# Sorted expert layer of a 12-layer decoder: down weights held in SBUF, rows loaded by fours, placing matmuls in bf16, and the last two batches' gathers and sums moved into the next stage

## The chip, the cores and the metric

The kernel runs on one core of a Trainium2 chip. The metric is the device time of one execution in microseconds (us). The core has TensorE (PE: matmuls; its weight loads are shown apart as PEld), VectorE (DVE), ScalarE (ACT), GpSimd (POOL) and SyncE (SP, which here only issues DMAs). POOL issues the indirect DMAs (gathers and scatters by a list of row numbers).

## The reference, cut to what matters

Twelve residual layers act on `x` of 4 batches x 512 tokens x 128 features. The third and the fourth matter here.

```python
def _L0_ffn_ref(x, gate_w, gate_b, w1, b1, w2, b2):      # 8 experts, top 2
    gate_logits = jnp.einsum('bsd,de->bse', x, gate_w) + gate_b
    weights, indices = jax.lax.top_k(gate_logits, TOP_K)
    weights = jax.nn.softmax(weights, axis=-1)
    h = jnp.einsum('bsd,edh->ebsh', x, w1) + b1[:, None, None, :]
    xh, gh = jnp.split(h, 2, axis=-1)
    act = jax.nn.silu(gh) * xh
    out_e = jnp.einsum('ebsf,efd->ebsd', act, w2) + b2[:, None, None, :]
    out_e = jnp.transpose(out_e, (1, 2, 0, 3))
    sel = jnp.take_along_axis(out_e, indices[..., None], axis=2)
    return jnp.sum(sel * weights[..., None], axis=2)

x = x + _L0_ffn_ref(_layernorm(x), ...)     # the sorted expert layer
x = x + _L1_attn_ref(_layernorm(x), ...)    # a gated scan along the tokens, per batch
```

The next layer, cross attention over 32 context tokens, shares a stage with the scan.

## The kernel before, in words

`x`, `y` and `a` live in SBUF, features on the 128 partitions, 2048 tokens along the free side; a batch is 512 columns (`sl(b)`). The program is a row of stages; each ends with a barrier over all engines, and at some of them the semaphores are cleared too. Within a stage every engine runs its own list in the order in which the code stands, and waits on semaphores; nothing is reordered.

`layer2` is the sorted expert layer. It computes only the two chosen experts of each token. Batches 0 and 1 are group 0, batches 2 and 3 group 1.

- *Choosing and placing.* TensorE centres the tokens and computes the gate logits; DVE ranks the experts (`choose`) and writes a 0/1 matrix `oh` of the chosen ones. `place(g)` counts with one matmul against a triangular matrix and eight against ones how many earlier tokens chose the same expert. DVE's `locate(g)` turns this into `where` (the row of each token and choice in a list that is sorted by expert, each expert's part filled up to a multiple of 128) and into `first_row` (for each tile of 128 rows the row at which its expert's weights begin in DRAM). POOL then scatters the normalised tokens, 16 indirect DMAs per group, into the DRAM tensor `sorted`.
- *The expert loop.* There are 23 tiles of 128 rows per group, N = 46 in all. For tile n: `turn` transposes four tiles at once on TensorE, ACT copies them (`lay`); `inner(n)` does four gate and four up matmuls, ACT applies Silu, DVE multiplies (`hidden`), `down(n)` does four down matmuls, DVE evicts (`evict`), and SP stores the 128 result rows to DRAM (`results`). TensorE's order is: turn of the next four (at n % 4 = 1), `inner(n)`, `down(n-1)`, and at n = 2, 4, 6, 8 a `flip` of the mixing weights of one batch (four small transposes).
- *Weights.* `ring(n)` is a ring of four slots in the big SBUF buffer. SP's `fetch(n)` reads the tile's expert from `first_row` and loads gate, up and down weights and biases, 128 x 1544 floats. `fetch(n+4)` waits for `down(n)`. On SP's queue it is followed by the store of tile n, which waits for its eviction.
- *Rows.* `bring(0)` loads four tiles, then the other 19 of group 0; `bring(1)`, at n = 10, loads the 23 tiles of group 1 in one DMA.
- *Coming back.* When a group's results are stored, POOL gathers for each of its 8 token tiles the two rows (16 indirect DMAs). `mix(b)` on DVE weights and adds them (eight instructions), `join(b)` on TensorE transposes them and adds the bias product (10 passes), `add(b)` on DVE adds to `x`. Batches 0 and 1 do this inside the expert loop, at n = 36 and 41; batches 2 and 3 (`last`) after it.

`layers_3_and_4` is the next stage. For each batch: `centre` (TensorE), `square` (ACT), `variance` (TensorE), `invert` (ACT: two Ln, two Exp), `normed` (DVE: `a` and `y`), POOL's `x += y`, `project_in` (four matmuls), `sigmoids` (ACT, with another function table), `scan` (DVE), `project_out` (TensorE), `add` (DVE). The batches are interleaved by the order of the code. Cross attention follows. The buffer `big` is 18,432 columns wide; `load_big` fills it in later layers, and `k.big_loaded` counts these loads.

Of the kernel before, what the change touches and what calls it, by code (L numbers as in the profile page):

```python
# [8 lines left out]
ALU = mybir.AluOpType  # L9
ACT = mybir.ActivationFunctionType  # L10
AX = mybir.AxisListType
F32 = mybir.dt.float32
# [10 lines left out]
MAGIC = 12582912.0  # L23
EXPERT_GROUPS = ((0, 1), (2, 3))
# [752 lines left out]
def layer2(nc, k, x, y, a):  # L777
# [5 lines left out]
    G, C, SLOTS, FOUR, W_COLS = 8, 4, 4, 4, 12 * P + 8  # L783
# [5 lines left out]
    turns = -(-N // FOUR)  # L789
    MIX_AT = {firsts[g + 1] + 13 + 5 * i: b for g, group in enumerate(EXPERT_GROUPS[:-1]) for i, b in enumerate(group) if firsts[g + 1] + 13 + 5 * i < N - 1}  # L790
    last = [b for b in range(B) if b not in MIX_AT.values()]
    names = ("bias_in counted numbered folded cg_ready zeroed centred squared summed rooted rs_ready logits chosen placed mapped normed exps shifted weighed "
             "positions turned laid gate up silu hidden down evicted flipped flat mixed joined done chain "
             "w_0 w_1 w_2 w_3 scattered_0 scattered_1 x_first x_in_0 x_in_1 stored_0 stored_1 stored_2 stored_3 got_0 got_1 got_2 got_3")
    rows_in, rows_out = k.sorted_rows, [nc.dram_tensor(f"results_{nc.next_id()}", (n * P, D), F32).ap() for n in limits]
    with ExitStack() as mem, stage(nc, names) as (block, s):
        sb = lambda n, w_, dt=F32: mem.enter_context(nc.sbuf_tensor(f"{n}_{nc.next_id()}", [P, w_], dt))
        cg, sq, var, b2, w8t = sb("cg", G), sb("sq", 2 * S), sb("var", NT), sb("b2", P), sb("w8t", T)
# [5 lines left out]
        where, spot, first_row, share = sb("where", 2 * NT, I32), sb("spot", 2 * NT), sb("first_row", N, I32), sb("share", 2 * NT)  # L804
        xt, out, o = sb("xt", 2 * S), sb("out", 4 * P), sb("o", 2 * S)
# [8 lines left out]

        @block.sync
        def _(sp):
            def fetch(n):
                g = group_of(n)
                sp.wait_ge(s["mapped"], g + 1)
# [4 lines left out]
            def bring(g):  # L824
                sp.wait_ge(s[f"scattered_{g}"], 16 * 2 * len(blocks[g]))
                for lo, hi, loaded in ((0, FOUR, "x_first"), (FOUR, limits[0], "x_in_0")) if g == 0 else ((0, limits[g], f"x_in_{g}"),):
                    dst = k.big[:, (firsts[g] + lo) * P:(firsts[g] + hi) * P].rearrange("p (n d) -> p n d", d=D)
                    sp.dma_start(dst, rows_in[g][lo * P:hi * P, :].rearrange("(n p) d -> p n d", p=P)).then_inc(s[loaded], 16)
# [6 lines left out]
            fetch(SLOTS - 1)  # L835
            for n in range(N):
                if n == 10 and len(EXPERT_GROUPS) > 1:
                    bring(1)
                if n + SLOTS < N:
                    fetch(n + SLOTS)  # L840
                g = group_of(n)
                sp.wait_ge(s["evicted"], n + 1)
                sp.dma_start(rows_out[g][sl(n - firsts[g], P), :], out[:, sl(n % 4, P)]).then_inc(s[f"stored_{n % 4}"], 16)
# [2712 lines left out]
```

## Time and profile before

| | us |
|---|---|
| three executions | 2023.61, 2015.76, 2008.88 |
| median | 2015.76 |
| the profiled execution | 2025.27 |
| its span on the core | 2023.2 |
| mean granted clock of TensorE, share of full | 0.928 |

| engine | busy us | share of the span | instructions |
|---|---|---|---|
| PE | 1777.6 | 88% | 20105 |
| PEld | 1285.1 | 64% | 20124 |
| DVE | 1241.8 | 61% | 2434 |
| ACT | 1056.1 | 52% | 2386 |
| POOL | 834.2 | 41% | 1087 |

How to read it: shares are averages over some fifty stages with different limits. A stage is read from the order of time in it: who waits last and for whom. A row of the timeline has the start in us, the duration of the whole group, the engine, the line of the kernel, the operation, out<-in with the shapes, how many instructions are in the group, and in brackets how long the engine stood idle before it and what released it. An fp32 matmul appears as two passes, each with a weight load.

### The profile page before, as it was taken

To read this page: it belongs to the slowest core of one execution; us is meant where nothing else is said; L and a number is where in the kernel's file an instruction comes from. 1 tells how busy PE (TensorE), PEld (TensorE's weight loads), DVE (VectorE), ACT (ScalarE), POOL (GpSimd) and SP (SyncE) were. 2 spreads that over 40 slices of the span, in tenths; PEclk is the share of its full clock that TensorE was granted. 3 is DMA by queue.
4 is the path that set the end of the run, shared out by engine and by line. 5 is a ranking of instruction groups with operands and counts; after the bars stand their busy time and mean duration, and the time that the engine had idled before them with its cause. 6 is when DMAs were issued, how large, how long until landed. Compare 5 with 4: busy or idle time off the path is not lost. (4 is left out here: it accounts for less than half of the span.)

```text
span 2023.2 us, 50650 instructions
## 1 busy us (share of the span) xinstructions
PE 1777.6 (88%) x20105; PEld 1285.1 (64%) x20124; DVE 1241.8 (61%) x2434; ACT 1056.1 (52%) x2386; POOL 834.2 (41%) x1087
## 2 busy tenths in 40 slices
PE   7784899485699999999999788999999999999885
PEld 4333898243457888888888536888788856633332
DVE  4544345259657777777674327887888777734434
ACT  4551443267686666666664344555555541066552
POOL 1004120305357776767662104666666620044201
PEclk9996999695799999999999798999999998799998
DMA  6003887000041000000000314444444300000100
GB/s 236 1 1 98 288 274 243 24 1 0 1 154 38 14 24 14 24 14 24 14 22 16 153 47 120 126 131 135 125 125 132 119 1 1 1 1 1 38 1 22
DMA packets 46846, 141.84 MB, mean 70 GB/s; under 512 B 11112, under 2 KB 17648, under 8 KB 45840
## 3 DMA queue, kind: packets, MB, share of 16 engines
q1 hardware_dynamic: 42704, 131.20, 20.0%
q0 software_dynamic: 2816, 7.21, 1.1%
q8 instruction: 164, 2.69, 0.5%
q14 instruction: 74, 0.61, 0.1%
q10 hardware_dynamic: 1088, 0.13, 0.0%
HBM read 120.43 MB, written 18.09 MB: 68 GB/s over the span
## 5 line engine op out<-in xcount | busy, mean ns | idle before, releaser
L2510 DVE SCALAR_TENSOR_TENSOR big<-bank,pack,big 128x256 f32<-128x256 f32 (+2 forms) x384 | 182.9, 477 | 41.6 <-ACT mask L2399 25.4
L1958 DVE TENSOR_TENSOR hl<-bank,hh 128x512 fp32r<-128x512 f32 x192 | 132.8, 692 | 64.6 <-ACT hh L1892 55.1
L1892 ACT ACTIVATE hh<-bank 128x512 fp32r<-128x512 f32 x192 | 114.9, 598 | 94.0 <-DVE bank L1953 90.9
L2398 ACT ACTIVATE big<-bank,pack 128x256 f32<-128x256 f32 x192 | 90.6, 472 | 127.8 <-PE bank L2206 123.4
L772 PE MATMUL bank<-yh,wl 128*128 128x512 f32 x384 | 151.4, 394 | 5.3 <-DVE yl L1902 2.5
L773 PE MATMUL bank<-yl,wh 128*128 128x512 f32 x384 | 150.6, 392 | 0.0
L774 PE MATMUL bank<-yh,wh 128*128 128x512 f32 x384 | 150.2, 391 | 0.0
L1792 POOL TENSOR_TENSOR a<-a,rep 128x512 f32<-128x512 f32 x96 | 125.0, 1302 | 30.7 <-DMA rep<-routing 25.6
L1953 DVE TENSOR_TENSOR bank<-bank,a 128x512 f32<-128x512 f32 x192 | 133.2, 694 | 6.6 <-POOL a L1792 0.9
L2910 ACT ACTIVATE pt<-bank 128x1024 f32<-128x1024 f32 (+3 forms) x128 | 79.5, 706 | 99.1 <-PE bank L2762 99.0
L2116 POOL TENSOR_TENSOR big<-big,mask 128x256 f32<-128x256 f32 (+1 forms) x128 | 93.7, 732 | 90.3 <-DVE big L2510 58.1
L2692 POOL TENSOR_SCALAR_AFFINE_SELECT pt<-pt 128x256 f32<-128x256 f32 x128 | 54.9, 440 | 175.4 <-ACT pt L2910 173.1
L2206 PE MATMUL bank<-y,pack 128*128 128x262 f32 (+1 forms) x384 | 120.5, 399 | 5.1 <-DVE big L2510 4.8
L2193 PE MATMUL bank<-big 128*128 128x128 f32 x896 | 123.6, 286 | 0.0
L1781 POOL CAST wh<-big 128x384 fp32r<-128x384 f32 x96 | 48.6, 506 | 169.3 <-PE bank L774 114.6
L2193 PEld LDWEIGHTS bank<-big 128*128 128x128 f32 x896 | 107.8, 192 | 5.2 <-issue 1.4
L1092 DVE SCALAR_TENSOR_TENSOR a<-bank,big,a 128x128 f32<-128x128 f32 x184 | 51.8, 344 | 95.4 <-ACT a L1005 87.1
L2936 DVE TENSOR_REDUCE part<-bank 128x8 f32<-128x1024 f32 (+1 forms) x80 | 93.9, 1219 | 24.5 <-PE bank L2742 23.7
L1783 POOL TENSOR_TENSOR wl<-big,wh 128x384 fp32r<-128x384 f32 x96 | 98.3, 1024 | 7.7
L2742 PE MATMUL bank<-big 32*128 32x128 f32 (+1 forms) x1024 | 92.6, 355 | 4.2 <-DVE part L2936 4.2
L2742 PEld LDWEIGHTS bank<-big 32*128 32x128 f32 x1024 | 74.3, 222 | 33.0 <-issue 18.8
L1005 ACT ACTIVATE a<-bank,big 128x128 f32<-128x128 f32 x184 | 52.5, 368 | 74.2 <-PE bank L904 73.8
(597 smaller groups left out, 4551.2 us busy)
## 6 DMA issues: line engine op xcount, KB each, us to landing
big<-in_experts SPq DMA_DIRECT2D x46, 772.0 KB, 4.7
rep<-routing SPq DMA_DIRECT2D x64, 384.0 KB, 3.5
rep<-routing SPq DMA_DIRECT2D x64, 256.0 KB, 4.0
big<-in_big SPq DMA_DIRECT2D x1, 9216.0 KB, 25.7
gate<-big SPq DMA_DIRECT2D x32, 256.0 KB, 2.0
z<-gate SPq DMA_DIRECT2D x16, 512.0 KB
rep<-routing SPq DMA_DIRECT2D x64, 128.0 KB, 3.6
pack<-in_pack SPq DMA_DIRECT2D x1, 5846.5 KB, 21.2
```

The source lines that it names most:

```text
L772: nc.tensor.matmul(out, pl, dh[:, cur], start=start, stop=False)
L773: nc.tensor.matmul(out, ph, dl[:, cur], start=False, stop=False)
L774: return nc.tensor.matmul(out, ph, dh[:, cur], start=False, stop=stop)
L1783: nc.gpsimd.tensor_tensor(low, src, high.bitcast(F32), ALU.subtract).then_inc(s["w_low"], 1)
L1792: nc.gpsimd.tensor_tensor(spread_(m), spread_(m), spread(n), ALU.mult).then_inc(s["odd"], 1)
L1892: nc.scalar.activation(hh[:, sl((n - 1) % 3)], up_bank(n - 1), ACT.Copy).then_inc(s["high"], 1)
L1953: nc.vector.tensor_tensor(up_bank(n), up_bank(n), other, ALU.mult).then_inc(s["h"], 1)
L1958: nc.vector.tensor_tensor(hl[:, sl(n % 3)], up_bank(n), hh[:, sl(n % 3)].bitcast(F32), ALU.subtract).then_inc(s["low"], 1)
L2193: mm4 = lambda out, gr, left_, right: [nc.tensor.matmul(out[:, sl(h % GH, P)], left_(h), right(h), start=True, stop=True) for h in hs(gr)][-1]
L2206: nc.tensor.matmul(haloed(i)[:, :, 3 - halo:], k.w["L2_attn_qkv_w"][:, sl(m, P)], tokens, start=True, stop=True).then_inc(s["raw"], 1)
L2510: ins = nc.vector.scalar_tensor_tensor(out=d, in0=conv_in(i, back), scalar=weight(i, 3 - back), in1=d, op0=ALU.mult, op1=ALU.add)
L2742: mm = nc.tensor.matmul(both(at)[:, gl * S + c * w:][:, 0:w], qj[b][rows, j * S + i * P:][:, 0:P], kd[b][rows, key:key + w], start=kind != ...
```

## The change

- The down weights of all eight experts (`big0`, 128 x 4096 floats, 2 MB) are loaded once, at the program's start, into columns 14336 to 18431 of `big`, as the last DMA of that stage on SP. A fetch now brings 128 x 1032 floats. `down(n)` reads the weights at a column that stands in a register: `first_col`, written by DVE beside `first_row`, is loaded by TensorE into 23 registers per group (`address(0)` ahead of the loop, `address(1)` at n = 4). `fetch(n+4)` waits for `hidden(n)`.
- Rows are loaded four tiles at a time, `bring(q)`, two turns ahead.
- `oh`, the triangle and the ones are bf16 in `place`; POOL writes the two bf16 copies.
- The flips move to n = 5, 7, 9, 11, and DVE's `weigh` to n = 1 and 3 of the loop.
- For batches 2 and 3 the gathers, `mix`, `join` and `add` move into the next stage: POOL issues the sixteen gathers ahead of its `x += y`; the batches there are centred one after the other, each after its late sum.

```diff
-    G, C, SLOTS, FOUR, W_COLS = 8, 4, 4, 4, 12 * P + 8
+    G, C, SLOTS, FOUR, W_COLS = 8, 4, 4, 4, 8 * P + 8
...
-        oh = [sb("oh", (len(bs) + 1) * G) for bs in blocks]
+        oh = [sb("oh", (len(bs) + 1) * G, BF16) for bs in blocks]
+        later_bf, ones_bf = sb("later_bf", P, BF16), sb("ones_bf", P, BF16)
...
+        down_weights = k.big[:, BIG0_AT:BIG0_AT + G * C * P]
...
+        def collect(pool, b):
+            g = [b in group for group in EXPERT_GROUPS].index(True)
+            for slot in range(4):
+                pool.wait_ge(late.s[f"stored_{slot}"], 16 * len(range(slot, firsts[g + 1], 4)))
+            for t in range(TB * b, TB * b + TB):
+                for i in range(2):
+                    nc.gpsimd.indirect_dma_start(out=found(t, i), out_offset=None, in_=rows_out[g], in_offset=bass.IndirectOffsetOnAxis(where[:, i * NT + t:][:, 0:1], 0)).then_inc(late.s[f"got_{b}"], 16)
...
             def fetch(n):
-                after(sp, s["down"], n - SLOTS + 1)
+                after(sp, s["hidden"], C * (n - SLOTS + 1))
...
+            def bring(q):
+                for g in range(len(blocks)):
+                    lo, hi = max(FOUR * q, firsts[g]), min(FOUR * (q + 1), firsts[g + 1])
+                    if lo < hi:
+                        sp.wait_ge(s[f"scattered_{g}"], 16 * 2 * len(blocks[g]))
+                        src = rows_in[g][(lo - firsts[g]) * P:(hi - firsts[g]) * P, :].rearrange("(n p) d -> p n d", p=P)
+                        sp.dma_start(k.big[:, lo * P:hi * P].rearrange("p (n d) -> p n d", d=D), src).then_inc(s[f"x_{q % 3}"], 16)
...
             bring(0)
             fetch(SLOTS - 1)
+            bring(1)
             for n in range(N):
-                if n == 10 and len(EXPERT_GROUPS) > 1:
-                    bring(1)
                 if n + SLOTS < N:
                     fetch(n + SLOTS)
+                if n % FOUR == 0 and n // FOUR + 2 < turns:
+                    bring(n // FOUR + 2)
+                store(n)
...
+            def address(g):
+                held = [pe.alloc_register(f"column_{n}_{nc.next_id()}") for n in range(firsts[g], firsts[g + 1])]
+                pe.wait_ge(s["addressed"], g + 1)
+                pe.load(held, first_col[0:1, 32 * g:32 * g + limits[g]])
+                columns.extend(pe.snap(r, min_val=0, max_val=(G - 1) * C * P) for r in held)
...
-                    mm = nc.tensor.matmul(down_bank(n), h(n, c), ring(n)[:, sl(2 * C + c, P)], start=c == 0, stop=c == C - 1)
+                    mm = nc.tensor.matmul(down_bank(n), h(n, c), down_weights[:, bass.ds(columns[n] + c * P, P)], start=c == 0, stop=c == C - 1)
...
         @block.gpsimd
         def _(pool):
+            for b in late.batches:
+                late.collect(pool, b)
             for b in range(B):
                 pool.wait_ge(s["y_ready"], b + 1)
...
+            def late_rows(b):
+                pe.wait_ge(s["kcopied"], 1)
+                late.join(pe, b)
+                pe.wait_ge(late.s["done"], b + 1)
...
             scan(0)
             scan(1)
+            late.mix(dve, 2)
             add(0)
+            late.add(dve, 2)
+            add(1)
             normed(2)
-            add(1)
+            scan(2)
+            late.mix(dve, 3)
+            late.add(dve, 3)
+            add(2)
             normed(3)
-            scan(2)
             scan(3)
-            add(2)
             add(3)
...
+                sp.dma_start(k.big[:, BIG0_AT:BIG0_AT + ap["big0"].shape[1]], ap["big0"]).then_inc(k.big_loaded, 16)
```

On TensorE's list, the expert loop's tiles 2 and 3 in the kernel before (L904 gate, L908 up, L915 down, L922 flip; each row is an instruction of the program, x4 four in a row):

```order
L904 MATMUL bank<-xt,big 128x128 x4
L908 MATMUL bank<-xt,big 128x128 x4
L915 MATMUL bank<-big,a 128x128 x4
L922 MATMUL bank<-pack,w_1486 8x128 x4
L904 MATMUL bank<-xt,big 128x128 x4
L908 MATMUL bank<-xt,big 128x128 x4
L915 MATMUL bank<-big,a 128x128 x4
```

The same place in the kernel after (L948 gate, L952 up, L965 down, L958 the register load of group 1): tile 3's gate and up, the down matmuls of tile 2, and the start of tile 4:

```order
L948 MATMUL bank<-xt,big 128x128 x4
L952 MATMUL bank<-xt,big 128x128 x4
L965 ISA
L965 MATMUL bank<-big,a 128x128
L965 ISA
L965 MATMUL bank<-big,a 128x128
L965 ISA
L965 MATMUL bank<-big,a 128x128
L965 ISA
L965 MATMUL bank<-big,a 128x128
L958 TENSOR_LOAD first_col
L959 ISA x3
```

Each down matmul has a register instruction (ISA) ahead of it, and one load of 23 registers stands between the down matmuls of tile 2 and the gate matmuls of tile 4.

On POOL's list, from the scatters (L859) to the adds of the next stage (L1163), before (L865 the gathers; L46 and L37 the end of the stage):

```order
L859 DMA sorted<-y,where 2944x128 x32
L865 DMA big<-results,where 128x128 x32
L46 UNCONDITIONAL_BRANCH
L37 ISA
L1159 UNCONDITIONAL_BRANCH
L1163 TENSOR_TENSOR x<-x,y 128x512 x4
```

And after (L906 the scatters, L828 the gathers, L1203 the adds):

```order
L906 DMA sorted<-y,where 2944x128 x32
L828 DMA big<-results,where 128x128 x16
L47 UNCONDITIONAL_BRANCH
L38 ISA x2
L1197 UNCONDITIONAL_BRANCH
L828 DMA big<-results,where 128x128 x16
L1203 TENSOR_TENSOR x<-x,y 128x512 x4
```

Sixteen of the thirty-two gathers stand behind the stage's end now, ahead of the four adds.

On TensorE's list in the scan stage, before (L1169 centre, L1174 variance, L1179 and L1185 the products of project_in, L1194 project_out):

```order
L1179 MATMUL bank<-a,pack 128x512 x2
L1169 MATMUL bank<-x,pack 128x512
L1179 MATMUL bank<-a,pack 128x512
L1185 MATMUL bank<-a,pack 128x512
L1179 MATMUL bank<-a,pack 128x512 x2
L1169 MATMUL bank<-x,pack 128x512
L1174 MATMUL bank<-sq,pack 128x512
L1194 MATMUL bank<-h,pack 128x512
L1174 MATMUL bank<-sq,pack 128x512
L1194 MATMUL bank<-h,pack 128x512
```

And after (L1209 centre, L1214 variance, L1219 and L1225 project_in, L1234 project_out, L833 and L835 the join):

```order
L1234 MATMUL bank<-h,pack 128x512
L833 MATMUL bank<-w8t,b_1441 128x512
L835 MATMUL bank<-pack,o 128x128 x4
L1209 MATMUL bank<-x,pack 128x512
L1214 MATMUL bank<-sq,pack 128x512
L1234 MATMUL bank<-h,pack 128x512
L1219 MATMUL bank<-a,pack 128x512
L1225 MATMUL bank<-a,pack 128x512
L1219 MATMUL bank<-a,pack 128x512 x2
L833 MATMUL bank<-w8t,b_1441 128x512
L835 MATMUL bank<-pack,o 128x128 x4
L1209 MATMUL bank<-x,pack 128x512
```

Batches 2 and 3 each have a join ahead of their centre, and batch 3's centre stands behind batch 2's products.

## Rows read from the trace of the kernel before

**Rows 1.** Stretches: busy us (count) per engine, granted clock, DMA share, GB/s.

```profile
198.50:353.00 154.50, 141.86 (x1178) 136.95 (x1178) 65.92 (x247) 62.62 (x201) 27.58 (x29) 0.96 0.81 270
355.00:386.00 31.00, 8.12 (x20) 4.55 (x20) 5.89 (x18) 0.00 (x0) 15.21 (x16) 0.54 0.12 36
388.00:440.00 52.00, 43.12 (x115) 18.89 (x115) 23.14 (x34) 35.70 (x55) 5.08 (x4) 0.96 0.00 0
```

**Rows 2.** Timeline: group 0's placing matmuls, and POOL's first scatter.

```profile
166.66 0.67 PE L884 MATMUL bank<-oh,pack 128*128 128x72 f32 x2 [1.13 <-DVE oh L1031]
167.13 3.52 PE L887 MATMUL bank<-oh,pack 128*128 128x64 f32 x16
173.76 1.08 POOL L859 DMA_INDIRECT sorted<-y,where  x1 [15.15 <-DVE where L1065]
```

**Rows 3.** Groups by line, TensorE: busy us, mean ns | idle before.

```profile
L1523 PE MATMUL bank<-q2w,q2t 128*128 128x128 bf16 x64 | 8.0, 285 | 0.4 <-ACT q2t L1613 0.3
L915 PE MATMUL bank<-big,a 128*128 128x128 f32 x368 | 49.6, 278 | 0.5 <-DVE a L1092 0.5
```

**Rows 4.** Timeline, TensorE: tile 1's turn.

```profile
205.00 0.63 PE L894 MATMUL bank<-pack,big 128*128 128x128 f32 x4 [0.86 <-DMA big<-sorted]
```

**Rows 5.** Timeline, TensorE: gate groups of tiles 1, 37, 38, 44, 45.

```profile
205.46 1.06 PE L904 MATMUL bank<-xt,big 128*128 128x128 f32 x8
...
322.40 1.06 PE L904 MATMUL bank<-xt,big 128*128 128x128 f32 x8
...
327.22 1.06 PE L904 MATMUL bank<-xt,big 128*128 128x128 f32 x8
...
347.10 1.06 PE L904 MATMUL bank<-xt,big 128*128 128x128 f32 x8
...
349.78 1.06 PE L904 MATMUL bank<-xt,big 128*128 128x128 f32 x8
```

**Rows 6.** Timeline, SP and TensorE: around the second group's rows, gates of tiles 13, 14, 16.

```profile
237.08 0.72 SPq L828 DMA_DIRECT2D big<-sorted  x1
...
238.76 4.83 SPq L822 DMA_DIRECT2D big<-in_experts  x1
...
241.43 1.13 PE L904 MATMUL bank<-xt,big 128*128 128x128 f32 x8 [0.15 <-issue]
...
249.35 2.05 PE L904 MATMUL bank<-xt,big 128*128 128x128 f32 x8 [5.00 <-issue]
...
257.59 1.06 PE L904 MATMUL bank<-xt,big 128*128 128x128 f32 x8
```

**Rows 7.** The fetches: three first on the timeline; line L822's durations and landing.

```profile
174.75 2.83 SPq L822 DMA_DIRECT2D big<-in_experts  x3
...
L822 SPq FUSED_REGOPS  x46: 37/37/48, 174.6 to 342.7; - x46
DMA to landing us min/median/max: 4.2/4.7/10.5
```

**Rows 8.** Timeline: from tile 45's eviction to the scan stage's last add.

```profile
354.31 0.29 DVE L1097 COPY out<-bank 128x128 f32<-128x128 f32 x1 [1.05 <-PE bank L915]
356.87 0.95 POOL L865 DMA_INDIRECT big<-results,where  x1 [49.75 <-DMA results<-out]
...
368.22 0.28 DVE L1105 TENSOR_SCALAR o<-big,share 128x128 f32<-128x128 f32 x1 [13.62 <-DMA big<-results,where]
...
375.71 0.95 POOL L865 DMA_INDIRECT big<-results,where  x1 [0.31 <-issue]
...
385.43 0.69 DVE L1111 TENSOR_TENSOR x<-x,bank 128x512 f32<-128x512 f32 x1 [4.23 <-PE bank L932]
...
387.96 3.75 PE L1169 MATMUL bank<-x,pack 128*128 128x512 f32 x4 [2.56 <-PEq L38]
...
403.35 0.69 DVE L1389 TENSOR_TENSOR h<-h,gt 128x512 f32<-128x512 f32 x1
...
426.58 0.69 DVE L1394 TENSOR_TENSOR x<-x,bank 128x512 f32<-128x512 f32 x1 [1.28 <-PE bank L1194]
```

More of the change, by code:

```diff
@@ L23 @@
 MAGIC = 12582912.0
+BIG0_AT = 14336
 EXPERT_GROUPS = ((0, 1), (2, 3))
@@ L813, in layer2, with join, mix, add @@
         mine = lambda m, g, w_=G: m[:, blocks[g][0] * w_:(blocks[g][-1] + 1) * w_]
+        def collect(pool, b):
[5 more added lines that the diff above has]
+                    nc.gpsimd.indirect_dma_start(out=found(t, i), out_offset=None, in_=rows_out[g], in_offset=bass.IndirectOffsetOnAxis(where[:, i * NT + t:][:, 0:1], 0)).then_inc(late.s[f"got_{b}"], 16)
+        def join(pe, b):
+            pe.wait_ge(late.s["mixed"], b + 1)
+            after(pe, late.s["done"], b)
+            nc.tensor.matmul(k.ps[7], b2[0:G, :], w8t[0:G, sl(b)], start=True, stop=False)
+            for i in range(TB):
+                mm = nc.tensor.matmul(k.ps[7][:, sl(i, P)], o[:, b % 2 * S + i * P:][:, 0:P], k.ident, start=False, stop=i == TB - 1)
+            mm.then_inc(late.s["joined"], 1)
+        def mix(dve, b):
+            dve.wait_ge(late.s[f"got_{b}"], 16 * 2 * TB)
+            after(dve, late.s["joined"], b - 1)
+            for i in range(TB):
+                t = TB * b + i
+                cur = o[:, b % 2 * S + i * P:][:, 0:P]
+                nc.vector.tensor_scalar(cur, found(t, 0), share[:, t:t + 1], None, ALU.mult).then_inc(late.s["scaled"], 1)
+                dve.wait_ge(late.s["scaled"], t + 1)
+                mixed = nc.vector.scalar_tensor_tensor(out=cur, in0=found(t, 1), scalar=share[:, NT + t:][:, 0:1], in1=cur, op0=ALU.mult, op1=ALU.add)
+            mixed.then_inc(late.s["mixed"], 1)
+        def add(dve, b):
+            dve.wait_ge(late.s["joined"], b + 1)
+            nc.vector.tensor_tensor(x[:, sl(b)], x[:, sl(b)], k.ps[7], ALU.add).then_inc(late.s["done"], 1)
+        late.collect, late.join, late.mix, late.add, late.batches = collect, join, mix, add, last
         @block.sync
@@ L923, in flip @@
                 mm.then_inc(s["flipped"], 1)
-            def join(b):
-                pe.wait_ge(s["mixed"], b + 1)
-                pe.wait_ge(s["flat"], B)
-                pe.wait_ge(s["bias_in"], 16)
-                after(pe, s["done"], b)
-                nc.tensor.matmul(k.ps[7], b2[0:G, :], w8t[0:G, sl(b)], start=True, stop=False)
-                for i in range(TB):
-                    mm = nc.tensor.matmul(k.ps[7][:, sl(i, P)], o[:, b % 2 * S + i * P:][:, 0:P], k.ident, start=False, stop=i == TB - 1)
-                mm.then_inc(s["joined"], 1)
+            columns = []
             nc.tensor.matmul(k.ps[7][:, 0:G], k.w["centre"], k.w["L0_ffn_gate_w"], start=True, stop=True).then_inc(s["folded"], 1)
@@ L943, in _ @@
             pe.wait_ge(s["normed"], B)
+            address(0)
+            pe.wait_ge(k.big_loaded, 16)
             turn(0)
             for n in range(N + 1):
+                if n == 4 and len(blocks) > 1:
+                    address(1)
                 if n % FOUR == 1 and n // FOUR + 1 < turns:
@@ L1121, in _ @@
                 shifted(g)
-            for g in range(len(EXPERT_GROUPS)):
-                weigh(g)
             for n in range(N + 1):
+                if n in (1, 3) and n // 2 < len(EXPERT_GROUPS):
+                    weigh(n // 2)
                 if n < N:
@@ L1129, in _, with layers_2_to_4, layers_3_and_4 @@
                 if n in MIX_AT:
-                    mix(MIX_AT[n])
+                    mix(dve, MIX_AT[n])
                 if n - 2 in MIX_AT:
-                    add(MIX_AT[n - 2])
-            for i, b in enumerate(last):
-                mix(b)
-                if i:
-                    add(last[i - 1])
-            add(last[-1])
-            dve.wait_ge(s["done"], B)
-def layers_3_and_4(nc, k, x, y, a):
+                    add(dve, MIX_AT[n - 2])
+            dve.wait_ge(s["evicted"], N)
+def layers_2_to_4(nc, k, x, y, a):
+    late = Kit()
+    names = "stored_0 stored_1 stored_2 stored_3 got_0 got_1 got_2 got_3 scaled mixed joined done"
+    late.s = {n: nc.alloc_semaphore(f"{n}_{nc.next_id()}") for n in names.split()}
+    with ExitStack() as mem:
+        layer2(nc, k, x, y, a, mem, late)
+        layers_3_and_4(nc, k, x, y, a, late)
+    counted.extend(late.s.values())
+def layers_3_and_4(nc, k, x, y, a, late):
     sems = ("centred squared var ln inv y_ready a_ready mixed keys values kcopied vcopied gates value sig driven gated proj summed "
```

114 lines of the change are left out of this document (53 added, 61 removed).

## Prediction

> **What bounds the kernel now.** I read the page first for the whole, then the busy time by stretch, then the order of time from 158 us (the sorted expert layer begins) to 428 us (the scan of the next stage ends). Everything the change touches lies there; the other 1,750 us I take as unmoved. Three things are to be seen. In the expert loop (198.5 to 353 us) TensorE is busy 141.9 of 154.5 us with its clock almost always at the upper level, 2.4 GHz (granted 0.96), while the DMA engines are busy 0.81 of the time: TensorE bounds it, DMA is close behind [rows 1]. Between 355 and 386 us almost nothing works but POOL, which issues sixteen gathers; TensorE is busy 8.1 of 31 us at the lower level, 1.2 GHz (0.54) [rows 1]. Before the loop, POOL's scatters wait until DVE has written `where`, and DVE waits for the placing matmuls [rows 2].
>
> **The loop's stalls.** The gate matmuls of two neighbouring tiles start 347.10 and 349.78: 2.68 us for 24 weight-and-matmul passes, 0.112 us each [rows 5]. The 45 gate groups from tile 1 (205.46) to tile 45 (349.78) span 144.3 us. Without stalls it would be 44 x 2.68 = 117.9; ten turns and four flips of four passes, 14 x 0.45 = 6.3; two joins, the first of which stretches a step from 2.68 to 4.82 (2.1), the second taken as 2.6, so 4.7. That makes 128.9, so **15.4 us are stalls**. Over half is one event: SP issues the whole second group's rows at 237.08 (1.4 MB in 512-byte rows), its next fetch is stuck in issue for 4.83 us, and tile 14's gate starts 7.92 us after tile 13's, after 5.00 us of idleness; by tile 16 the loop is 16.16 us from tile 13 where 8.04 would do: 8.1 us lost, part of it because TensorE's clock fell to the lower level after the idle time (the gate group at 249.35 takes 2.05 us, the one at 257.59 1.06) [rows 6]. The rest is weights that land late: a fetch needs 4.7 us (4.2 to 10.5) to land [rows 7] and is issued only after `down(n)`.
>
> **The change, part by part** (gains positive).
> 1. *Places in bf16.* Per group one L884 and eight L887 matmuls, 18 passes in fp32, from 166.66 to 170.65: 4.0 us [rows 2]. In bf16 they are 9 passes. Bounds: half of it, 2.0; or nine at 8.0/64 = 0.125 us, the bf16 row of 128x128 [rows 3], 1.1, so 2.9 saved. That row is the nearer in type, but it stands at the upper clock level and this stretch at the lower: I take 2.6. For group 0 it is on the path (place, `where`, first scatter at 173.76, the rest of the scatters, first rows). Group 1's copy is hidden, since POOL is busy with group 0's scatters until about 194. The extra `first_col` instruction and the two bf16 copies on POOL lie beside waits. **+2.6** (2.0 to 2.9).
> 2. *Rows by fours.* Tile 1's turn waited 0.86 us for the 19-tile load [rows 4]; it goes, but the turn then comes nearer to the low clock of the start: **+0.5** (0 to 0.9). The second group's 23-tile burst disappears altogether.
> 3. *Down weights in SBUF.* A fetch falls from 772 to 516 KB. It no longer waits for `down(n)` but for `hidden(n)`. The SP queue still has `store(n-1)` ahead of it, so it comes only about 1 us sooner. With a transfer two thirds as long, the weights that were late by tenths come over 1 us early. The 2 MB load at the start sits at the end of SP's queue, 150 us ahead of its use: 0, covered by layers 0 and 1. With the burst and the lateness both gone I take 14 of the 15.4: **+14** (8 to 15.4; 8 if only the burst goes).
> 4. *Registers on TensorE.* Two `TENSOR_LOAD`s of 23 registers. The first stands in the 12 us in which TensorE waits for rows: 0. The second stands in the loop ahead of tile 4 and stops what is queued behind it, tile 4's gate. The trace has only SP's load of one register: three fetches in 2.83 us, (2.83 - 0.33)/2 - 0.33 - 0.04 = 0.88 us each [rows 7]. Bounds: 0.88 for the lot, or 23 x 0.88 = 20. About 2 us is covered, because the sequencer gets there when `hidden(2)` is done while the third down group is still to run. So the cost is 0 to 18; the nearest row is one load instruction, so I stay near it but not on it: **-3**.
>  The Trainium skill (Runtime: NRT & Kernel Launch, Instruction fetch mechanics) speaks against this edit: a register load costs some 200 ns per register even in bulk, by which each load would be an estimated 4.6 us and the second would cost 2.6. No row of this case shows a bulk load.
> 5. *A register operation ahead of each down matmul*, 4 x 46 = 184. SP's takes 37 ns [rows 7]: 0 if TensorE's sequencer runs ahead, 6.8 us if not. `hidden(n)` is ready about 1.2 us before its down group's turn, longer than four such operations: **0**.
>  The Trainium skill (TensorE: Matmul & The Clock Gate, Architectural detail) gives TensorE's queue a depth of 64, by which a step's instructions are ahead of the array; that too makes it 0.
> 6. *The last two batches inside the scan stage.* Before: tile 45's eviction ends at 354.59, the first gather starts at 356.87, the mix at 368.22, the last sum ends at 386.12, the new stage starts at 387.96, and its last `add` ends at 427.27: 72.7 us after the eviction [rows 8]. After: 1.8 us of barrier, then from the stage's start 0.5 + 16 x 1.256 = 20.6 us until POOL has issued the gathers (fifteen steps from 356.87 to 375.71). Behind them on POOL stand its own adds `x += y` (5.08/4 = 1.27 each [rows 1]), which DVE's `add(0)` needs, and behind `add(0)` on DVE stands `late.add(2)`, which `centre(2)` on TensorE needs: centre(2) at about 23.7. Batch 0 in the trace goes from centre (387.96) to gated (404.04) in 16.1 us, with the keys' work and four microseconds of low clock in it [rows 8]; alone on fast matmuls its own instructions sum to about 11. I take 12. Then batch 3's mix (eight instructions, 2.6), join (2.1, as in the loop) and add (0.7), 5.4 together, its chain 12, its output product and add 2: 23.7 + 12 + 5.4 + 12 + 2 = 55.1; with 16.1 twice, 63.3. One batch at a time leaves TensorE gaps, so I put 58. 72.7 - 1.8 - 58 = 12.9, less 1 since the second normalisation now starts right behind the last batch instead of beside it: **+12** (6 to 15).
>
> Sum: 2.6 + 0.5 + 14 - 3 + 0 + 12 = **26 us**. Against the profiled execution's 2025.3 us that is 1999; it stands 9.5 us above the median of three, 2015.8 (range 2008.9 to 2023.6), so I forecast 2015.8 - 26 = **1990 us**.
>
> **Rivals.**
> A. *POOL's queue and the clock eat the overlap.* If centre(2) waits as worked out and TensorE's clock stays at the lower level through both chains, item 6 gives 6 or less: 1996 to 1999. For it: the stretch with sparse TensorE work had 0.54; against: from 388 on, with gaps of 1 to 2 us, it had 0.96 [rows 1].
> B. *Registers load one after another.* Item 4 costs 18 instead of 3, with a fall of the clock behind the idle time: 2006. For it, the only load in the trace costs 0.88 us; against, it is a single instruction.
> C. *More arrives*: the bulk load is hidden and item 6 gives 15: 1983 to 1978.
> D. *Slower.* A down matmul whose address stands in a register may not start until the pass before it has ended. A pass lasts 278 ns [rows 3] and its neighbours start every 112: 0.166 x 368 = 61 us more, 2015.8 - 26 + 61 = 2051. It decides from 26/368 = 0.07 us a pass. No row shows a matmul with a register address; against it, no wait in this trace hangs on how an address was made.
> E. *The loop was not held by its loads*: a rhythm of 2.68 us with the same stalls. Against it: the stalls sit exactly behind the burst. It would give 2004.
>
> **Chances.** Forecast 0.56, A 0.14, B 0.12, C 0.09, D 0.05, E 0.04. The forecast's own range is 1980 to 1999. The range for 8 in 10, which takes in A and C and part of B: 1976 to 2005. About 1% (20 us) is what a measurement of this kernel can tell from no change: 1995.6 is that line. Faster takes 0.47 of the forecast, all of C and half of A: 0.63. Slower by over 1% is D: 0.05. Same 0.32.
>
> **What would show it.** Right: the gate groups 2.68 us apart without a gap near tile 14; the first scatter 2.6 us sooner; gathers issued beside the scan stage's first matmuls; `centre(2)` released by DVE's sum about 24 us after the stage begins; the eviction of tile 45 to the stage's last add in about 60 us. Wrong: a TensorE gap over 3 us ahead of tile 4 (B); down groups longer than 1.06 us (D); the granted clock at 0.5 for most of the scan stage (A); fetches still landing late (E).

## The result, and the profile after

| | before | after |
|---|---|---|
| executions | 20 | 20 |
| median, us | 2010.32 | 1995.89 |
| lowest to highest, us | 1999.85 to 2025.28 | 1986.62 to 2010.86 |
| the profiled execution, us | 2025.27 | 1993.77 |
| its span, us | 2023.2 | 1992.0 |

The ratio over all executions is 0.9941, 95% interval 0.9918 to 0.9964 (0.9928 between the two medians): 0.6 to 0.7% faster, less than the 1% that a measurement tells from no change. The direction and the range of the forecast held, its size did not: 14 us between the medians instead of 26. The same pair gave 0.9894 (0.9856 to 0.9932) and 0.9916 (0.9881 to 0.9951) in two further comparisons (e1 and e10 below), so all three lie below 1.

The two profiled executions lie 31 us apart, more than twice as much as the medians. By stage, each from its start to the next one's, in us:

| stretch | before | after | |
|---|---|---|---|
| start of `layer2` to the first gate group | 42.4 | 39.2 | -3.2 |
| first gate group to tile 45's eviction | 154.2 | 139.7 | -14.6 |
| tile 45's eviction to the end of the scan and cross attention stage | 94.0 | 93.1 | -0.9 |
| sum | 290.6 | 271.9 | -18.7 |
| one attention layer late in the program | 331.4 | 316.0 | -15.4 |
| all the rest | 1401.2 | 1404.1 | +2.9 |

The attention layer's code is untouched. Its largest group by line of before, and then of after (busy us, mean ns | idle before):

```profile
L2742 PE MATMUL bank<-big 32*128 32x128 f32 (+1 forms) x1024 | 92.6, 355 | 4.2 <-DVE part L2936 4.2
```

```profile
L2794 PE MATMUL bank<-big 32*128 32x128 f32 (+1 forms) x1024 | 80.8, 314 | 4.1 <-DVE part L2988 4.1
```

In before's trace TensorE's granted clock is 0.77 from 1665 to 1785 us, so it stands for part of the layer at 1.2 GHz; in after's it is 0.93. Over all thirteen traces of the study this mean is 314 or 315 ns in seven, 332 in one and 345 to 355 in five, with either kernel on either side. So that part is not the change's; it belongs to the execution. **The change's own share is the 18.7 us**, which came out as 18.5 in a second pair of traces.

*Ahead of the loop*, timeline of after (start, duration, engine, line, operation, [idle before, releaser]):

```profile
166.09 0.19 PE L928 MATMUL bank<-oh,later_bf 128*128 128x72 bf16 x1 [1.13 <-DVE oh L1077]
166.12 0.35 PE L931 MATMUL bank<-oh,ones_bf 128*128 128x64 bf16 x8
...
167.06 0.21 DVE L1102 TENSOR_TENSOR full<-bank,number 128x64 f32<-128x64 f32 x1
...
170.06 1.08 POOL L906 DMA_INDIRECT sorted<-y,where  x1 [11.56 <-DVE where L1111]
```

The placing matmuls take 0.4 us where they took 4.0 [rows 2]; DVE no longer waits for them, and the first scatter comes 12.6 us after the layer's start instead of 15.8.

*The loop.* TensorE's rows by line (duration ns min/median/max), and the fetches' landing:

```profile
L958 PEldq TENSOR_LOAD <-first_col x2: 2329/2432/2535, 179.5 to 207.5; - x2
...
L965 PE MATMUL bank<-big,a x368: 275/275/372, 202.7 to 335.6; 128*128 x184
L965 PEldq FUSED_REGOPS  x184: 46/46/56, 201.7 to 335.1; - x184
...
DMA to landing us min/median/max: 3.4/4.1/5.9
```

Timeline, TensorE: ahead of tile 4, and the gates of tiles 13 and 16:

```profile
208.06 1.06 PE L965 MATMUL bank<-big,a 128*128 x8
210.79 1.13 PE L948 MATMUL bank<-xt,big 128*128 128x128 f32 x8 [1.68 <-issue]
...
238.04 1.06 PE L948 MATMUL bank<-xt,big 128*128 128x128 f32 x8
...
246.08 1.06 PE L948 MATMUL bank<-xt,big 128*128 128x128 f32 x8
```

Tiles 13 to 16 are 8.04 us apart, without a gap, where before lost 8.1 [rows 6]. A fetch lands after 4.1 us instead of 4.7, and never later than 5.9 instead of 10.5 [rows 7]. The one idle time over 0.6 us in the loop is that of the register load ahead of tile 4. The down matmul whose address stands in a register has a median of 275 ns, which is also the median of before (mean 278 [rows 3]).

*The last two batches*, busy us per engine, granted clock, DMA share and GB/s by stretch, and the timeline:

```profile
338.40:358.20 19.80, 16.36 (x36) 6.90 (x36) 7.31 (x10) 12.89 (x20) 14.51 (x15) 0.85 0.18 46
358.20:369.00 10.80, 4.20 (x11) 2.43 (x11) 6.83 (x12) 0.94 (x1) 3.44 (x3) 0.64 0.05 14
369.00:383.00 14.00, 9.47 (x14) 2.87 (x14) 4.77 (x7) 7.14 (x10) 1.26 (x1) 0.79 0.00 0
383.00:394.00 11.00, 7.91 (x15) 4.04 (x16) 2.81 (x10) 0.81 (x2) 0.00 (x0) 0.60 0.00 0
```

```profile
335.95 0.29 DVE L1144 COPY out<-bank 128x128 f32<-128x128 f32 x1 [1.14 <-PE bank L965]
...
338.39 3.75 PE L1209 MATMUL bank<-x,pack 128*128 128x512 f32 x4 [2.48 <-PEq L39]
...
339.15 0.95 POOL L828 DMA_INDIRECT big<-results,where  x1 [46.28 <-SPq L47]
...
358.23 0.95 POOL L828 DMA_INDIRECT big<-results,where  x1 [0.30 <-issue]
...
359.04 2.73 DVE L844 TENSOR_SCALAR o<-big,share 128x128 f32<-128x128 f32 x1
359.19 2.49 POOL L1203 TENSOR_TENSOR x<-x,y 128x512 f32<-128x512 f32 x2
...
363.84 0.68 DVE L1442 TENSOR_TENSOR x<-x,bank 128x512 f32<-128x512 f32 x1
364.02 2.04 PE L833 MATMUL bank<-w8t,b 8*128 8x512 f32 x2 [5.96 <-issue]
...
365.99 2.08 PE L835 MATMUL bank<-pack,o 128*128 128x128 f32 x8
...
368.10 0.69 DVE L851 TENSOR_TENSOR x<-x,bank 128x512 f32<-128x512 f32 x1 [3.58 <-PE bank L835]
...
368.84 2.07 PE L1209 MATMUL bank<-x,pack 128*128 128x512 f32 x2 [0.78 <-DVE x L851]
...
385.31 2.04 PE L833 MATMUL bank<-w8t,b 8*128 8x512 f32 x2 [4.03 <-issue]
...
390.13 2.07 PE L1209 MATMUL bank<-x,pack 128*128 128x512 f32 x2 [0.78 <-DVE x L851]
...
407.32 0.69 DVE L1442 TENSOR_TENSOR x<-x,bank 128x512 f32<-128x512 f32 x1 [1.22 <-PE bank L1234]
```

The 33.4 us between eviction and new stage [rows 8] have become 2.1, and the stage is 30.3 us longer. Batch 2 is centred 30.5 us after the stage's start, batch 3 another 21.3 us later, and the last add ends 71.8 us after the eviction, against 72.7 before. TensorE is busy 4.2 of 10.8 us from 358 on, and from then to 394 its clock is between the levels or near the lower one.

### The profile page after: what moved, and what is told of

It is laid out like the page before. It is cut to its first block and busy times, and to the rows that moved or that the text cites. A ratio compares the mean times of both kernels' runs of the same rounds, so it can differ in the third digit from the quotient of the medians.

```text
span 1992.0 us, 50826 instructions
## 1 busy us (share of the span) xinstructions
PE 1758.3 (88%) x20087; PEld 1263.7 (63%) x20106; DVE 1242.2 (62%) x2436; ACT 1062.5 (53%) x2388; POOL 835.3 (42%) x1089
## 5 line engine op out<-in xcount | busy, mean ns | idle before, releaser
L2010 DVE TENSOR_TENSOR hl<-bank,hh 128x512 fp32r<-128x512 f32 x192 | 132.9, 692 | 65.2 <-ACT hh L1944 55.7
L773 PEld LDWEIGHTS bank<-yh,wl 128*128 128x128 f32 x384 | 72.8, 189 | 28.8 <-issue 4.7
L2794 PE MATMUL bank<-big 32*128 32x128 f32 (+1 forms) x1024 | 80.8, 314 | 4.1 <-DVE part L2988 4.1
```

What stands on the lines that cost most here:

```text
L773: nc.tensor.matmul(out, pl, dh[:, cur], start=start, stop=False)
L2010: nc.vector.tensor_tensor(hl[:, sl(n % 3)], up_bank(n), hh[:, sl(n % 3)].bitcast(F32), ALU.subtract).then_inc(s["low"], 1)
```

## The experiments

Every label is a whole kernel. The landmarks of each trace in us: the loop from the first gate group to tile 45's eviction; from that eviction to the scan stage's last add; and from it to that stage's end. Runs e1 to e4 were made on one chip, e5 to e8 on a second, e9 to e11 on a third; on the first two the loop has two long stalls, in the kernel before too (e4; last section), so loops are compared among e1 to e8 alone, and with care: there the same loop differs by 2 to 3 us from trace to trace (166.0, 168.1 and 168.7 for that of after).

| kernel | loop | to the last add | to the stage's end |
|---|---|---|---|
| before | 154.2 | 72.7 | 94.0 |
| after | 139.7 | 71.8 | 93.1 |
| e4 before, again | 182.0 | 72.3 | 93.7 |
| e1 after, again | 166.0 | 71.4 | 92.7 |
| e2 old tail | 168.6 | 74.2 | 95.6 |
| e3 late sums only | 181.0 | 72.7 | 94.0 |
| e5 fours only | 178.5 | 73.2 | 94.5 |
| e6 burst, small fetches | 176.1 | 74.3 | 95.7 |
| e7 POOL's adds wait | 168.1 | 67.8 | 89.1 |
| e8 fillers | 168.7 | 65.2 | 86.7 |
| e9 early mix | 139.3 | 54.8 | 76.2 |
| e10 after, a third time | 139.4 | 71.7 | 93.1 |
| e11 early mix and fillers | 139.0 | 54.6 | 76.1 |

**After and before once more.** No edit.

> The kernel after once more, for the spread. S is the stretch from the start of the expert layer to the end of the scan and cross attention stage; it was 290.6 us in the trace of before and 271.9 in that of after. Theory T (the gain is the loop's, the late batches give nothing): S 271 to 273 again, ratio to before 0.994. Rival R (the stalls of the one trace of before were unusual, S differs little in general): S still 272, but before's S nearer 280 in a new trace.

> The kernel before once more, one look. Theory T: the burst of the second group's rows stalls the loop again, tiles 13 to 16 in about 16 us, and S is 288 to 293. Rival R: the stall is smaller by more than half, S below 285.

After: 2025.21 us median of 6, ratio 0.9894 (0.9856 to 0.9932). Loop minus 16.0, the two stages together 299.4 against 317.9, minus 18.5. The shares by stage repeat; the whole time of both kernels is 1 to 2% longer on this chip.

**The old tail on the kernel after** (item 6 undone), **and the new tail alone on the kernel before.**

```diff
 e2, on after:
-            scan(1)
-            late.mix(dve, 2)
-            add(0)
-            late.add(dve, 2)
+            for i, b in enumerate(last):      # at the end of layer2 again, with its
+                mix(dve, b)                   # gathers and joins; the scan stage's
...                                            # lists are those of before
 e3, on before: item 6 as in the diff above, and the flips at their new places
```

> The kernel after without the move of batches 2 and 3: their gathers and sums stand at the expert layer's end again and the scan stage has its old order. Theory T: the loop keeps its gain and the old tail costs the same, 94.0 us from tile 45's eviction to the end of the stage as in the trace of before, so S is 178.8 + 94.0 = 273 and the ratio is that of after, 0.994. The forecast's item 6 (the move is worth 12 us): S 284, ratio 1.000.

> The kernel before with the move of batches 2 and 3 alone: fp32 places, whole fetches, rows in bursts. Theory T: S 289 to 291, as before, ratio 1.000 within 0.003. Item 6 as forecast: S 278, ratio 0.994.

e2: 2022.56 us median of 8 (2021.81 without the highest), ratio 0.9914 (0.9872 to 0.9956), beside 2025.21 us and 0.9894 for the kernel after; e3: 2048.47 us, ratio 1.0008 (0.9973 to 1.0044). Added to before, item 6 changes nothing; on the other parts it takes 2.8 us off the way from the eviction to the stage's end (95.6 to 92.7), and that is less than the times can tell. The old tail alone spreads as far from trace to trace (93.7 to 95.7 us to the stage's end in before, e2, e4, e5 and e6; the new one 92.7 to 94.0 in after, e1, e3 and e10). So the gain is that of the other parts, and the 12 us of item 6 did not come.

**Rows by fours alone; small fetches with the burst kept.**

```diff
 e5, on before: rows by fours (the flips at their new places in both)
+            bring(1)
             for n in range(N):
-                if n == 10 and len(EXPERT_GROUPS) > 1:
-                    bring(1)
+                if n % FOUR == 0 and n // FOUR + 2 < turns:
+                    bring(n // FOUR + 2)
 e6, on before: down weights in SBUF, the bursts stay
-    G, C, SLOTS, FOUR, W_COLS = 8, 4, 4, 4, 12 * P + 8
+    G, C, SLOTS, FOUR, W_COLS = 8, 4, 4, 4, 8 * P + 8
```

> The kernel before with the rows loaded by fours alone: whole fetches of 772 KB that wait for the down matmuls, fp32 places, old tail. The loop from tile 0's gate to tile 45's eviction took 154.2 us in before and 139.7 in after. Theory: more than half of the 15 us is the burst, so about 145 to 146 here, with stalls of 1 to 2 us left at late weights. Rival (the size of the fetches is the cause): 150 or more.

> The kernel after with the rows in bursts again, fp32 places and the old tail: small fetches of 516 KB that wait for the hidden rows. Theory: the burst still blocks the queue, but there is less ahead of it: 145 to 148 us for the loop, with one gap of 3 to 5 us near tile 14. Rival (the size of the fetches is the cause): 140 to 142.

The loops are 178.5 and 176.1 us. On the same chip the kernel after has 168.1 and 168.7 (e7 and e8, whose edits lie behind the loop), so each half alone is 7 to 10 us short of both together; against before's 182.0, from the other disturbed chip, e5 gives 3.5 and e6 5.9 where both give 16.0. The lengths that were expected were those of an undisturbed loop and can't be held against these. But that more than half of the gain would be the burst's is not borne out: e5, which takes away the burst, gives the smaller part, if by little more than the loops' spread.

What is left in each is seen on the timeline. e5, TensorE, no gap at the second group's rows, but stalls elsewhere (a step that holds a turn or a flip is 3.12 us long by itself, 2.68 + 0.44). The first pair below is 3.16 us apart with no turn between, so 0.5 us is lost; ahead of the last row the engine was idle for 1.90 us, and 1.80 again 13 us later. Before has such a gap too, 1.92 us at 294.42, and after has none. That these are weights of 772 KB that land late is likely, but this run's profile has no landing times:

```profile
263.06 1.06 PE L946 MATMUL bank<-xt,big 128*128 128x128 f32 x8
...
266.22 1.13 PE L946 MATMUL bank<-xt,big 128*128 128x128 f32 x8 [0.32 <-issue]
...
291.18 1.13 PE L946 MATMUL bank<-xt,big 128*128 128x128 f32 x8 [1.90 <-issue]
```

e6, SP and TensorE, at the burst:

```profile
256.42 0.73 SPq L867 DMA_DIRECT2D big<-sorted  x1
...
258.01 2.57 SPq L861 DMA_DIRECT2D big<-in_experts  x1
...
265.74 1.13 PE L944 MATMUL bank<-xt,big 128*128 128x128 f32 x8 [1.61 <-issue]
```

The fetch behind the burst is stuck in issue for 2.57 us instead of 4.83 [rows 6], and the gap is 1.6 us instead of 5.0. Each half takes away a part of the stalls, and only with both (after, e10) are none left.

**POOL's adds held back until batch 2 is mixed.**

```diff
                 late.collect(pool, b)
+            pool.wait_ge(late.s["mixed"], 3)
             for b in range(B):
```

> The kernel after with POOL's adds held back until DVE has mixed batch 2. In the trace of after one of DVE's mixing instructions took 2.73 us, 0.28 otherwise, while POOL added. Theory (the two engines shut each other out of SBUF): the longest is 0.28 to 0.4 us, the mix ends 2.4 us sooner, POOL's adds come 1 to 2 us later and the late sum about 1 us sooner or the same. Rival (the long instruction is an accident of the record): it is long again.

Timeline of DVE, POOL and TensorE:

```profile
388.90 0.28 DVE L844 TENSOR_SCALAR o<-big,share 128x128 f32<-128x128 f32 x1
...
391.49 2.49 POOL L1204 TENSOR_TENSOR x<-x,y 128x512 f32<-128x512 f32 x2 [1.09 <-DVE o L846]
...
394.83 2.07 PE L1210 MATMUL bank<-x,pack 128*128 128x512 f32 x2 [0.78 <-DVE x L851]
```

The first instruction of the mix takes 0.28 us instead of 2.73. Batch 2 is centred 25.5 us after the stage's start instead of 30.5, and the last add 67.8 us after the eviction instead of 71.4 to 71.8 (the three traces of the kernel after), more than the 1 us that was expected. One wait more, and it is faster: POOL's adds had shut DVE out. Not all of it is that, though. Of the 5.0 us at batch 2's centre, 2.4 are the mix's (2.5 us instead of 4.9), 1.5 the join's, which now ran in part at the upper clock level (2.5 instead of 4.05), and 1.2 lie ahead of the mix, where the new wait does not act yet. It is one trace.

**Fillers: fifteen matmuls that compute nothing that is used**, where TensorE waits.

```diff
             project_out(0)
+            pe.wait_ge(s["kcopied"], 1)
+            fill(6)
             late_rows(2)
...
             project_out(1)
+            fill(2)
             project_in(2)
+            fill(4)
             late_rows(3)
...
             variance(3)
+            fill(3)
```

> The kernel after with 15 matmuls in the scan stage whose result nobody reads, in front of the two joins and the two projections, so that TensorE does not stand idle. Stage start to the last add took 69.7 us in after, clock 0.60 to 0.85 in parts. Theory (the low clock is a good part of what item 6 lost): the clock stays at 0.95 or more, joins take 2.3 us instead of 4.1, centres 1.1 instead of 2.1, and the last add ends at 60 to 64 us. Rival (the serial order alone is the cause): 68 to 71.

Timeline, TensorE: the fillers, the join, and the centres of batches 2 and 3:

```profile
387.53 5.31 PE L1284 MATMUL bank<-a,pack 128*128 128x512 f32 x12
394.49 1.09 PE L833 MATMUL bank<-w8t,b 8*128 8x512 f32 x2 [1.64 <-issue]
395.51 1.16 PE L835 MATMUL bank<-pack,o 128*128 128x128 f32 x8
397.45 1.65 PE L1209 MATMUL bank<-x,pack 128*128 128x512 f32 x2 [0.78 <-DVE x L851]
...
416.93 1.13 PE L1209 MATMUL bank<-x,pack 128*128 128x512 f32 x2 [0.78 <-DVE x L851]
```

The join's groups take 1.09 and 1.16 us instead of 2.04 and 2.08, and the last add comes 65.2 us after the eviction, 6.2 less than in e1. The clock did not stay at 0.95 as expected (0.83 from 400 to 414 us, 1.00 from 414 to 425). Measured from the stage's start, batch 2's centre comes only 0.9 us sooner than in after: the mix starts 3.5 us later there (DVE's last product of `scan(1)` starts only at 390.43; why, the profile does not show), and no longer meets POOL's adds. The rest comes with batch 3, where the clock is up: mix, join and add take 5.4 us instead of 7.3, and its chain from centre to gated 12.1 instead of 16.0. So about 6 us of the lost gain are the clock's, in the order of the kernel after.

**Early mix: the same work in another order.**

```diff
-            for b in late.batches:
-                late.collect(pool, b)
+            late.collect(pool, 2)
             for b in range(B):
+                if b == 1:
+                    late.collect(pool, 3)
                 pool.wait_ge(s["y_ready"], b + 1)
...
             project_in(0)
+            pe.wait_ge(s["kcopied"], 1)
+            late.join(pe, 2)
             project_in(1)
             project_out(0)
-            late_rows(2)
+            pe.wait_ge(late.s["done"], 3)
             centre(2)
...
             normed(1)
+            late.mix(dve, 2)
             scan(0)
+            late.add(dve, 2)
             scan(1)
-            late.mix(dve, 2)
             add(0)
-            late.add(dve, 2)
             add(1)
```

Batch 3 is treated in the same way, one step later.

> The kernel after with the late sums put where nothing waits for them: VectorE mixes batch 2 right behind normed(1) and adds it behind scan(0), TensorE joins batch 2 behind project_in(0), GpSimd adds y of batch 0 between the gathers of batches 2 and 3 instead of behind all sixteen. Theory O (item 6 fell through the order: centre(2) stands behind sixteen gathers, scans 0 and 1, POOL's adds and a join): centre(2) comes about 20 us after the stage's start instead of 30.5, the last add at 47 to 57 instead of 69.5, and the whole kernel is 12 to 20 us faster than the kernel after (ratio to before 0.980 to 0.985). Rival L (the chain of a batch, some 14 to 16 us at the lower clock level, twice, decides alone): centre(2) comes sooner, but the last add still stands above 62 and the gain is below 7 us.

> The kernel after, beside the run above on one chip: ratio to before 0.989 to 0.994, eviction of tile 45 to the scan stage's last add 71.8 us, and, if the two long stalls of the expert loop seen on the second chip belong to that chip, a loop of 140 us from the first gate group to the last eviction; if they come and go on one chip, 166.

e9: 1986.87 us median of 6, ratio to before 0.9834 (0.9786 to 0.9881); beside it the kernel after 2001.36 us median of 12, 0.9916 (0.9881 to 0.9951). The last add ends 54.8 us after the eviction instead of 71.7. So this order is faster than both kernels: against after by 14.5 us between the medians and 16.9 in the stage. Timeline of e9:

```profile
350.56 0.32 DVE L844 TENSOR_SCALAR o<-big,share 128x128 f32<-128x128 f32 x1
...
353.37 1.09 PE L833 MATMUL bank<-w8t,b 8*128 8x512 f32 x2 [1.01 <-issue]
...
355.76 0.68 DVE L851 TENSOR_TENSOR x<-x,bank 128x512 f32<-128x512 f32 x1
...
359.68 1.02 PE L1210 MATMUL bank<-x,pack 128*128 128x512 f32 x2
...
388.95 0.69 DVE L1446 TENSOR_TENSOR x<-x,bank 128x512 f32<-128x512 f32 x1 [1.22 <-PE bank L1235]
```

Batch 2's late sum is done at 356.4, beside the scans of batches 0 and 1, and its centre no longer waits for it; it comes 22.8 us after the stage's start (20 expected: `project_in(1)` and `project_out(0)` stand ahead of it on TensorE). That the second chain decides alone (rival L) is refuted. The joins run at the upper clock level now (1.09 us for L833), and the clock is 0.90 from 357 to 374 us and 0.89 from there to 390, with no filler.

**Early mix and twelve fillers.**

```diff
+            fill(3)
             late.join(pe, 2)
...
             project_out(1)
+            fill(2)
             project_in(2)
+            fill(4)
             late.join(pe, 3)
...
             variance(3)
+            fill(3)
```

> The early order and in addition 12 filler matmuls of 128x512 into a free bank (3 behind project_in(0), 2 behind project_out(1), 4 ahead of the join of batch 3, 3 behind its variance), which compute nothing that is used. Theory: the lower clock level costs part of the chain, as it did in the kernel after (last add 6.6 us sooner there with 15 fillers), so the last add comes 2 to 5 us sooner than in the early order alone. Rival: with TensorE busier by itself the clock is up already and the fillers cost their own 0.45 to 0.9 us each where something waits: 0 to 3 us later.

1980.46 us, ratio 0.9824 (0.9781 to 0.9866). The stretches of its scan stage:

```profile
338.40:358.70 20.30, 16.98 (x50) 7.67 (x51) 9.25 (x18) 11.65 (x18) 15.39 (x16) 1.00 0.16 43
358.70:376.00 17.30, 15.36 (x41) 6.34 (x40) 10.17 (x17) 9.56 (x13) 4.64 (x4) 1.00 0.04 11
376.00:391.00 15.00, 13.26 (x30) 4.79 (x29) 6.01 (x8) 8.44 (x12) 1.27 (x1) 1.00 0.00 1
```

The clock is at 2.4 GHz throughout, and yet the last add comes only 0.2 us sooner than in e9: 2 to 5 were expected and did not come. The four fillers ahead of batch 3's join cost about what the clock gives back (batch 3's chain from centre to gated, 12.1 us instead of 13.4): the join starts at 373.85, 35.5 us after the stage's start, and in e9 at 371.35, 34.5 us after.

## Why the prediction was right in direction and wrong in size

1. *Places in bf16*: right, 3.1 us at the first scatter instead of 2.6. The placing takes 0.38 us from its start to its end (166.09 to 166.47), a third of the 1.1 that I took for the shortest; it ends 3.6 us sooner after the layer's start, but DVE first has another instruction pair to finish (1.28 us from 165.86), and `full` starts right behind it. So only 3.1 of the 3.6 us arrive.
2. *Rows by fours* and 3. *down weights*: 14.5 us were forecast together. The loop gave 14.6 net of the register load's 1.8, so 16.4. From tile 1's gate to tile 45's it is 130.4 us instead of 144.3 [rows 5], 13.9 + 1.8 = 15.7: all the stalls counted (15.4), where I took 14 of them; the rest, 0.8, fell between tiles 0 and 1. Both mechanisms stood (e5, e6), and that the loop was not held by its loads (rival E) is refuted.
4. *Registers on TensorE*: 1.8 us instead of 3. Tile 4's gate stands 4.52 us behind tile 3's instead of 2.68. The load of 23 registers takes 2.33 and 2.54 us, 0.10 to 0.11 us each. Beside that row stands the rule of the Trainium skill (Runtime: NRT & Kernel Launch, Instruction fetch mechanics) of some 200 ns a register, which it states of loads from HBM (the chip's DRAM): this trace, where the registers come from an SBUF tile, does not agree, the load took about half of that. One after another at SP's 0.88 us (rival B) is refuted.
5. *A register operation ahead of each down matmul*: 0, as forecast; 184 of 46 ns lie hidden, and the pass stays at 275 ns. Rival D is refuted with it.
6. *The last two batches*: **this is the term that failed**: 12 forecast, 0.9 measured in the first pair; 2.8 (e1 against e2) and -0.3 (e3 against e4) to the stage's end. The barrier was nearly right (2.1 us instead of 1.8), and so was POOL: its queue is through with the gathers 20.8 us after the stage's start (20.6), and its adds take 1.25 each. The working, 23.7 + 12 + 5.4 + 12 + 2 = 55.1 us from the stage's start, came to 69.7, and these are the steps:
   - *centre(2) at 30.5 instead of 23.7, 6.8 us.* I had it released by POOL's adds through `add(0)`, as though the mix and the join were done by then. But on DVE `mix(2)` stands behind `scan(1)` and starts only at 359.04, though its eight gathers were issued by 348.9. It then takes 4.9 us instead of 2.6, since its first instruction runs into POOL's adds (2.73 us instead of 0.28), and TensorE's join comes behind that, 4.05 us at the lower clock instead of 2.1.
   - *batch 2 from centre to gated*: 14.0 instead of 12, 2.0 us.
   - *mix, join and add of batch 3*: 7.3 instead of 5.4 (390.13 - 382.87), 1.9 us, all of it the join at the lower clock.
   - *batch 3's chain*: 16.0 instead of 12, 4.0 us; the rest 0.1 less. I took 12 against a measured 16.1 in the trace of before, arguing that less would lie beside it and that the matmuls would be fast. They were not: with the clock up the chain does take 12.1 us (e8 and e11), so the 12 was right for the upper level alone. The value with 16.1 stood in the text and was the nearer one.

   6.8 + 2.0 + 1.9 + 4.0 - 0.1 = 14.6, and 55.1 + 14.6 = 69.7. My 58 had 2.9 of these in reserve, which leaves 11.7; 0.3 is the barrier's, and the 1 us that I took off for the second normalisation did not come (21.3 us from the last add to the stage's end in both traces): 12.0 - 11.7 - 0.3 + 1.0 = 1.0, and 0.9 was measured.

   How much of it is which cause, the runs say only in part: another order alone returns 17 us (e9), POOL's adds held back 3.6 (e7), a faster clock 6.2 in the order of the kernel after (e8) and 0.2 in the early order (e11). They overlap and must not be summed. I read the order as the first cause, since it opens the idle stretch of TensorE (5.96 us ahead of the join) behind which the clock is low; e9, which closes it, has 0.90 without a filler where after has 0.64 and 0.79. Rival A had the effect (item 6 gives 6 or less, 1996 to 1999) and half of the reason: the clock, but not POOL's queue, which kept to its time.

In sum, 18.7 us of stages instead of 26: item 1 plus 0.6, the loop plus 3.1, item 6 minus 11.1. The prediction subtracted from 2015.8, the median of three executions; over twenty it is 2010.3, so a forecast of 26 us would have meant 1984. Two errors of about 5 and 7 us, the base and the size, went opposite ways; that 1990 lies only 6 us from the measured 1995.9 is in part luck. The rest of the miss, some 4 us between 18.7 by stage and 14.4 by medians, has no cause that the runs show; the clock of the untouched attention layer moves a single execution by 10 to 15.

## What to carry to other kernels

Work moved beside other work gains nothing if the list of some engine still puts it behind that work: for each moved piece write down, engine by engine, which instruction stands ahead of it and when that one ends, not only when its data are there. Here the mix could start 13.7 us into the stage (e9) and DVE's list let it come at 20.7, and another order of the same instructions gave 17 us. When chains that used to lie side by side come one after another, take their length from rows at the clock level that they will have (here 12.1 us for one batch at the upper level, 16.0 as it ran), and expect TensorE, with gaps between the pieces, to lose the upper one.

## What the runs showed of the hardware that I had not expected

*A DVE instruction of 0.28 us took 2.73 us beside POOL.* L844 reads and writes SBUF alone, and so does POOL's add. In after by line, and in e7 the same instruction 0.28 us with POOL held back:

```profile
L844 DVE TENSOR_SCALAR o<-big,share x16: 277/280/2734, 305.3 to 384.5; 128x128 f32<-128x128 f32 x16
```

The Trainium skill (SBUF — State Buffer, SBUF: two separate sides) says that VectorE and GpSimd share one pair of ports as an exclusive lock that holds for a whole instruction, taken by VectorE in its two-port modes; the trace agrees, DVE being held from 359.04 to 361.77 and POOL's two adds lasting to 361.68. By the same section the one that starts first gets the pair, and there the rows differ: DVE's starts 0.15 us ahead of POOL's. In e9 it is seen again, at 366.80: one of the mix's L846 takes 1.26 us instead of 0.35 beside a single add of POOL (366.65 to 367.91).

*On two of the chips the expert loop was disturbed while POOL issued its indirect DMAs*, with the loop of either kernel. In e1 (its loop is 26 us longer than in the first trace of the same kernel) ScalarE, VectorE and TensorE wait:

```profile
216.08 2.26 ACT L1051 ACTIVATE a<-bank,big 128x128 f32<-128x128 f32 x8 [10.14 <-remote]
...
302.54 0.37 PE L952 MATMUL bank<-xt,big 128*128 128x128 f32 x1 [1.03 <-issue]
...
302.97 0.95 POOL L828 DMA_INDIRECT big<-results,where  x1 [0.30 <-issue]
...
306.96 1.12 DVE L1139 SCALAR_TENSOR_TENSOR a<-bank,big,a 128x128 f32<-128x128 f32 x4 [12.60 <-remote]
```

The first stall lies in the last scatters of group 1, the second in the gathers of group 0; in it TensorE's matmuls come one at a time, 1.4 us apart, with nothing in the profile that they wait for. The scan stage, with its sixteen gathers, is as long there as elsewhere. The cause stays open: no run varied it, and it went with the chip. It is why loops were compared within those chips alone.

*The clock of untouched code* differs from execution to execution, as the attention layer's group shows (314 to 355 ns). e9's profiled span, 1990.7 us, is only 4.3 shorter than e10's, although its scan stage is 16.9 shorter: it fell on 354 ns there, e10 on 314.
